# Cross attention: weighted values computed right behind a step's row phase, and their VectorE additions moved behind the row maxima

## Chip, cores and metric

One core of a Trainium2 chip runs the whole program. The metric is the device time in microseconds (us), the median of several runs. TensorE is called PE, its weight loads PEld, VectorE DVE, ScalarE ACT and GpSimd POOL.

## What is computed

A stream `x` of 32 batches of 64 tokens with 256 features goes through six layers. The first and the fourth are cross attentions with a context `ctx_512` of 1601 tokens and 128 features for each batch; the change touches these two alone.

```python
def _L0_xattn_ref(q, k, v, Wq, bq, Wk, bk, Wv, bv, Wo, bo):
    ...
    qh = (q @ Wq + bq).reshape(B, LQ, HEADS, D_K).transpose(0, 2, 1, 3)
    kh = (k @ Wk + bk).reshape(B, LKV, HEADS, D_K).transpose(0, 2, 1, 3)
    vh = (v @ Wv + bv).reshape(B, LKV, HEADS, D_K).transpose(0, 2, 1, 3)
    scale = 1.0 / np.sqrt(D_K)
    scores = jnp.einsum('bhqd,bhkd->bhqk', qh, kh) * scale
    attn = jax.nn.softmax(scores, axis=-1)
    out = jnp.einsum('bhqk,bhkd->bhqd', attn, vh)
    concat = out.transpose(0, 2, 1, 3).reshape(B, LQ, D_MODEL)
    return concat @ Wo + bo
...
    x = x + _L0_xattn_ref(_layernorm(x, axis=-1), ctx_512, ctx_512, L0_xattn_Wq, ...)
    x = x + _L0_attn_ref(...)
    x = x + _L0_ffn_ref(...)
    x = x + _L1_xattn_ref(_layernorm(x, axis=-1), ctx_512, L1_xattn_Wq, L1_xattn_Wkv, L1_xattn_Wo)
    x = x + _L1_attn_ref(...)
    x = x + _L1_ffn_ref(...)
```

There are 16 heads of 16 features, and the softmax subtracts the largest score of each row of a head before the exponential.

## The kernel before

`cross_attention` works through `STEPS` = 32 x 7 = 224 steps. Step `s` belongs to batch `u` and group `g` (`u, g = divmod(s, 7)`); a group is two tiles of 128 context tokens. Group 6 has one tile of 65 tokens, so its step is short. Each engine has its own program, a loop over the steps in a fixed order; the engines meet through semaphores alone.

PE does these blocks in step `s`, in this order:

- **Row phase (S)**, `scores(s)`: the scores of this step (L625) with the shift by the maximum (L631), and between them `largest` (L549), which computes in reduced precision the scores of the next batch, of which DVE takes the maxima. Both use 32 rows of the array for each of four strips. The phase opens with `largest` of the TRAIL strips 2 and 3, then come scores, and `largest` of the LEAD strips 0 and 1 stands near its end. ACT takes the exponentials of the scores (L805).
- **Keys (K)**, `project_keys` (L536), of the batch after: ACT copies them out (L708), POOL rounds them (L842).
- **Values (V)**, `project_values` (L568), of step `s + 2`: ACT copies them out (L716).
- In the last step of a batch **T**, `turn_maxes` (L557): the next batch's maxima are transposed and DVE copies them to `shift` (L920). For an even `u` above 0 the output projection **W**, `project_out` (L577), follows, which DVE adds to `x` (L966).
- **Weighted values (P)**, `weigh` (L596), of step `s - 1`: probabilities times values, 32 columns of the array for each strip. DVE's `gather` adds the result to `u_sb` (L974 in group 0, L977 in the others).

K, V, T, W, P and each of the four `largest` write to one of four PSUM banks, `misc_ps`, in turn. The list `ORDER`, filled by `step_ops(s)`, numbers these operations; number n uses bank n modulo 4, and `open_bank` makes PE wait until number n - 4 was read out by ACT (semaphore `act_free`) or DVE (`dve_free`):

```python
            def open_bank(op):
                if AT[op] >= NMB:
                    read_out(pe, ORDER[AT[op] - NMB])
                return bank(op)
```

The order of the blocks thus also says which read each block waits for. With M2, M3, M0, M1 for the four `largest` in program order, a plain step is M2, M3, M0, M1, K, V, P. K waits for the read of M2, V for M3, P for M0; in the next step M2 waits for M1, M3 for K (ACT), M0 for V (ACT) and M1 for P (DVE).

In group 0 the row phase also waits before its first score until DVE has copied `shift`: `read_out(pe, ("T", u))` (L619).

DVE takes in each step the four maxima (L910), then a share of the previous batch's division (`mask_odd` in group 2, `join_even` 3, `invert` 4, `divide` 5) or `keep_shift` in group 6, in the second cross attention also `later_tile` in the odd steps 3 to 25, and at last `gather`; `swap_halves` stands behind it in group 1.

Of the kernel before, what the change touches and what calls it, by code (L numbers as in the profile page):

```python
# [13 lines left out]
P = 128  # L14
# [203 lines left out]
def cross_attention(nc, tag, x_sb, ident, pair_mask, ctxT, wq, wk, wv, wo, bq, bv, bo, source=None, returned=None):  # L218
# [46 lines left out]
    def key_share(u, g):  # L265

        return (u + 1 + (g + 2) // NG, (g + 2) % NG)
# [4 lines left out]
    def step_ops(s):  # L272

        u, g = divmod(s, NG)
        ops = [("M", u + 1, g, j) for j in TRAIL + LEAD] if u + 1 < B else []
        if key_share(u, g)[0] < B:
            ops.append(("K",) + key_share(u, g))
        if s + 2 < STEPS:
            ops.append(("V", s + 2))
        if s in TURNED_AT:  # L280
            ops.append(("X", TURNED_AT[s]))
        if s in QUERIED_AT:
            ops.append(("Q", QUERIED_AT[s]))
        if s == 0 and bo is not None:
            ops.append(("C",))
        if g == NG - 1 and u + 1 < B:
            ops.append(("T", u + 1))
        if g == NG - 1 and u % 2 == 0 and u > 0:
            ops.append(("W", u // 2 - 1))
        if s > 0:  # L290
            ops.append(("P", s - 1))
        return ops

    ORDER = PROLOGUE + [op for s in range(STEPS) for op in step_ops(s)] + [("P", STEPS - 1), ("W", B // 2 - 1)]
# [8 lines left out]
    with ExitStack() as ctx:  # L303
# [170 lines left out]
        def _(pe):  # L474
# [5 lines that stand above are left out]
# [101 lines left out]
            def weigh(op):  # L581

                s = op[1]
                g = s % NG
                dst = open_bank(op)
                pe.wait_ge(exp_done, 2 * s + 2)
                if s == 0:
                    pe.wait_ge(filled, 1)
                read_out(pe, ("V", s))
                mine = tiles(g)  # L590
                for h, i in enumerate(mine):
                    for r in range(GROUPS):
                        c, half = r // 2, r % 2
                        at = ((h * KD + c) * 2 + half) * LQ
                        for j in range(QUADS):
                            ins = nc.tensor.matmul(  # L596
                                dst[j * 32:(j + 1) * 32, r * LQ:(r + 1) * LQ],
                                v_sb[0:keys(i), g, h, 4 * c + j, 2 * half:2 * half + 2, :].rearrange("p s d -> p (s d)"), probs[0:keys(i), s % 2, j, at:at + LQ],
                                start=h == 0 and r == 0, stop=h == len(mine) - 1 and r == GROUPS - 1, skip_group_check=True)
                ins.then_inc(misc_ready, 1)  # L600
# [77 lines left out]
            for s in range(STEPS):  # L678
                u, g = divmod(s, NG)
                scores(s)  # L680
                if key_share(u, g)[0] < B:
                    project_keys(("K",) + key_share(u, g))
                if s + 2 < STEPS:
                    project_values(("V", s + 2))
                if s in TURNED_AT:
                    turn_later(("X", TURNED_AT[s]))
                if s in QUERIED_AT:
                    project_queries(("Q", QUERIED_AT[s]))
                if s == 0 and bo is not None:
                    bias_row(("C",))  # L690
                if g == NG - 1 and u + 1 < B:
                    turn_maxes(("T", u + 1))
                if g == NG - 1 and u % 2 == 0 and u > 0:
                    project_out(("W", u // 2 - 1))
                if s > 0:
                    weigh(("P", s - 1))
            weigh(("P", STEPS - 1))
            project_out(("W", B // 2 - 1))

# [203 lines left out]
        def _(dve):  # L903
# [139 lines left out]
            for s in range(STEPS):  # L1043
                u, g = divmod(s, NG)
                if u + 1 < B:
                    for j in TRAIL + LEAD:
                        keep_max(("M", u + 1, g, j))
                if g == 2 and u > 0:
                    mask_odd(u - 1)
                if g == 3 and u > 0:  # L1050
                    join_even(u - 1)
                if g == 4 and u > 0:
                    invert(u - 1)
                if g == 5 and u > 0:
                    divide(u - 1)
                if s == 0 and bo is not None:
                    keep_bias(("C",))
                if g == NG - 1 and u + 1 < B:
                    keep_shift(("T", u + 1))
                if s in ADDED_AT:  # L1060
                    later_tile(ADDED_AT[s])
                if s == ROOTS_AT + 1 and returned is not None:
                    for j in range(1, TURNS):
                        invert_root(j)
                if g == NG - 1 and u % 2 == 0 and u > 0:
                    add_out(("W", u // 2 - 1))
                if s > 0:
                    gather(("P", s - 1))
                if g == 1 and u > 0:
                    swap_halves(u - 1)  # L1070
            gather(("P", STEPS - 1))
            swap_halves(B - 1)
            mask_odd(B - 1)
# [1838 lines left out]
```

## Time and profile before

| what | value |
|---|---|
| median of 3 runs | 3653.75 us (3653.49 to 3654.69) |
| profiled execution, its own time | 3656.24 us |
| its span | 3654.4 us, mean granted share of the PE clock 0.953 |
| PE busy | 3304.5 us (90%) |
| PE weight loads busy | 2671.3 us (73%) |
| DVE busy | 2496.6 us (68%) |
| ACT busy | 2194.2 us (60%) |
| POOL busy | 1474.0 us (40%) |

The span is that of the program's instructions on the core; the execution's own time holds it and the little that lies around it. The steps of the first cross attention lie from 46 to 973 us of the span, those of the second from 1629 to 2569 us. Matmuls overlap in the records, and the end of each is modelled; their starts are measured.

### The profile page before, as it was taken

The numbers are of one execution on the slowest core, as the hardware profiler recorded it, in microseconds if no ns is written. First come the engines' busy times: TensorE is split into PE (matmuls) and PEld (weight loads), VectorE is DVE, ScalarE is ACT, GpSimd is POOL, SyncE is SP. The second block draws the span as 40 slices with busy tenths as digits, with TensorE's granted clock in tenths as the row PEclk, the third lists the DMA queues.
The fourth block names the chain that finished last, engine by engine and source line by source line (L and its number), as shares of the span: only waits on it lengthen the run. The fifth ranks groups of instructions, "written<-read, shape, count | busy, mean of one in ns | idle before, by whom it ended". The sixth has DMA issues, their size and how long they took to land. (4 is left out here: it accounts for less than half of the span.)

```text
span 3654.4 us, 132188 instructions
## 1 busy us (share of the span) xinstructions
PE 3304.5 (90%) x56430; PEld 2671.3 (73%) x56431; DVE 2496.6 (68%) x4548; ACT 2194.2 (60%) x3465; POOL 1474.0 (40%) x1409
## 2 busy tenths in 40 slices
PE   9999999999886599979999999999867888888888
PEld 6888888888686466657888888888436666666667
DVE  5777777777545122248677777777669999999864
ACT  5666666666562122225766666666758888888632
POOL 4433333333132200045333333332029899999600
PEclk8999999999896799979999999999979999999989
DMA  2000001000005200011100100010001111111100
GB/s 80 31 31 31 31 31 40 31 31 22 11 2 215 101 32 31 30 65 58 33 30 31 31 31 31 31 40 4 27 17 50 44 47 46 45 47 47 36 25 23
DMA packets 60146, 147.51 MB, mean 40 GB/s; under 512 B 8210, under 2 KB 28466, under 8 KB 59218
## 3 DMA queue, kind: packets, MB, share of 16 engines
q1 hardware_dynamic: 56530, 131.04, 10.9%
q8 instruction: 442, 7.24, 0.8%
q0 software_dynamic: 3072, 8.39, 0.7%
q14 instruction: 102, 0.84, 0.1%
HBM read 122.63 MB, written 16.78 MB: 38 GB/s over the span
## 5 line engine op out<-in xcount | busy, mean ns | idle before, releaser
L805 ACT ACTIVATE x_probs<-x_score_ps 128x1024 f32<-128x1024 f32 (+1 forms) x896 | 815.1, 961 | 616.6 <-PE x_score_ps L631 588.7
L910 DVE TENSOR_REDUCE x_maxes<-x_misc_ps 128x1 f32<-128x512 f32 (+1 forms) x1792 | 1022.7, 627 | 36.3 <-PE x_misc_ps L549 30.7
L842 POOL CAST x_kT_hi<-x_kT 128x512 fp32r<-128x512 f32 (+1 forms) x448 | 254.2, 568 | 1141.1 <-ACT x_kT L708 1091.6
L2484 POOL TENSOR_TENSOR b_drive<-b_b_all,b_dtx 128x1024 f32<-128x1024 f32 x256 | 601.9, 2369 | 241.3 <-DVE b_dtx L2578 173.0
L2541 DVE TENSOR_TENSOR_SCAN b_state<-b_decay_ps,b_drive 128x512 f32<-128x512 f32 x512 | 598.9, 1212 | 33.9 <-POOL b_drive L2484 26.0
L625 PE MATMUL x_score_ps<-x_qz,x_kT 32*128 32x128 f32 x13312 | 592.9, 278 | 2.7 <-issue 2.2
L625 PEld LDWEIGHTS x_score_ps<-x_qz,x_kT 32*128 32x128 f32 x13312 | 502.3, 182 | 7.5 <-issue 5.1
L596 PE MATMUL x_misc_ps<-x_probs,x_v 128*32 128x64 f32 x26624 | 465.3, 221 | 1.1 <-issue 0.6
L596 PEld LDWEIGHTS x_misc_ps<-x_probs,x_v 128*32 128x32 f32 x26624 | 392.6, 110 | 78.6 <-issue 25.1
L2308 PE MATMUL b_turn_ps<-ident,b_state 128*128 128x128 f32 x2048 | 299.2, 288 | 153.7 <-DVE b_state L2541 97.3
L549 PE MATMUL x_misc_ps<-x_kT_hi,x_qz_hi 32*128 32x512 f32 (+1 forms) x2048 | 429.4, 405 | 5.5 <-DVE x_maxes L910 1.4
L2308 PEld LDWEIGHTS b_turn_ps<-ident,b_state 128*128 128x128 f32 x2048 | 230.7, 145 | 215.5 <-DVE b_state L2541 123.3
L2393 ACT ACTIVATE b_decay_ps<-b_dt,b_a_log 128x504 f32<-128x504 f32 x512 | 349.4, 683 | 63.2 <-DVE b_state L2541 62.6
L977 DVE TENSOR_TENSOR x_u<-x_misc_ps,x_u 128x256 f32<-128x256 f32 x384 | 162.9, 424 | 294.4 <-PE x_misc_ps L596 291.5
L631 PE MATMUL x_score_ps<-x_shift,x_ones 1*128 1x512 f32 (+1 forms) x1792 | 313.7, 456 | 0.5 <-issue 0.4
L2402 ACT ACTIVATE b_read<-b_turn_ps,b_c_turned 128x512 f32<-128x512 f32 x384 | 262.5, 684 | 72.5 <-PE b_turn_ps L2308 70.3
L716 ACT ACTIVATE x_v<-x_misc_ps 128x512 f32<-128x512 f32 (+1 forms) x448 | 260.4, 581 | 20.0 <-PE x_misc_ps L568 13.5
L708 ACT ACTIVATE x_kT<-x_misc_ps 128x512 f32<-128x512 f32 (+1 forms) x448 | 249.9, 558 | 16.0 <-PE x_misc_ps L536 15.4
L549 PEld LDWEIGHTS x_misc_ps<-x_kT_hi,x_qz_hi 32*128 32x128 f32 x2048 | 211.1, 185 | 64.3 <-DVE x_maxes L910 9.8
L394 POOL TENSOR_TENSOR x_raw_lo<-x_raw,x_raw_hi 128x512 fp32r<-128x512 f32 (+1 forms) x192 | 236.1, 1230 | 15.5
L568 PE MATMUL x_misc_ps<-x_wv_hi,x_raw_hi 128*128 128x256 f32 (+1 forms) x832 | 238.2, 286 | 0.0
L2314 PE MATMUL b_acc_ps<-ident,b_read 128*128 128x128 f32 x1536 | 235.0, 278 | 3.4 <-ACT b_read L2402 3.1
(318 smaller groups left out, 5777.6 us busy)
## 6 DMA issues: line engine op xcount, KB each, us to landing
x_raw<-in_ctxT SPq DMA_DIRECT2D x64, 800.5 KB, 4.5
b_b_all<-b_b_rows SPq DMA_DIRECT2D x128, 256.0 KB, 3.3
m_w<-in_m_w SPq DMA_DIRECT2D x16, 704.0 KB
m_w<-in_m_w SPq DMA_DIRECT2D x8, 768.0 KB
m_slot_rows<-m_zero SPq DMA_DIRECT2D x1, 4992.0 KB, 18.1
m_block_rows<-m_slot_rows SPq DMA_DIRECT2D x39, 128.0 KB, 2.0
m_slot_out<-m_out SPq DMA_DIRECT2D x39, 128.0 KB, 1.7
x<-in_x SPq DMA_DIRECT2D x4, 512.0 KB, 7.4
```

Of the source, the lines that this page charges most:

```text
L549: ins = nc.tensor.matmul(dst[:, m * kn:(m + 1) * kn], qz_hi[rows, b % 2, c, :, :].rearrange("p s q -> p (s q)"), kT_hi[rows, (b * NG + n) ...
L596: ins = nc.tensor.matmul(dst[j * 32:(j + 1) * 32, r * LQ:(r + 1) * LQ], v_sb[0:keys(i), g, h, 4 * c + j, 2 * half:2 * half + 2, :].rearran ...
L625: nc.tensor.matmul(score_ps[0:kn, j, n * P:(n + 1) * P], kT[rows, u % 2, c, cols(mine[h])], qz[rows, u % 2, c, :, :].rearrange("p s q -> p ...
L631: nc.tensor.matmul(score_ps[0:kn, j, 0:len(mine) * 2 * P], ones[j * 32:j * 32 + 1, 0:kn], shift[j * 32:j * 32 + 1, u % 2, :].rearrange("p ...
L716: nc.scalar.activation(v_sb[rows, g, 0:n, :, 0:4:3, :].rearrange("p a h s d -> p (a h) s d"), bank(op)[rows, 0:n * D].rearrange("p (a s d) ...
L805: nc.scalar.activation(probs[rows, s % 2, js, 0:n], score_ps[rows, js, 0:n], ACT.Exp).then_inc(exp_done, 1)
L910: nc.vector.tensor_reduce(maxes[:, c:c + m, j, k0 // NB], bank(op)[:, 0:m * even].rearrange("p (c k) -> p c k", c=m)[:, :, 0:kn], AX.X, AL ...
L2308: ins = nc.tensor.transpose(dst[:, c * P:(c + 1) * P], state[:, k % 2, c, i * P:(i + 1) * P], ident[:, :])
L2393: nc.scalar.activation(by_sequence(decay_ps[:, c % 2, :])[:, :, inside(p)], by_sequence(dt[:, p % 2, c, :])[:, :, inside(p)], ACT.Exp, sca ...
L2402: nc.scalar.activation(read[:, r, :], bank(use), ACT.Copy, scale=c_of(k, READ[r])).then_inc(act_free, 1)
L2484: nc.gpsimd.tensor_tensor(drive[:, h % 3, :, :], b_all[:, k % 2:k % 2 + 1, :].broadcast_to([P, 2, NB]), dtx[:, half * 2:half * 2 + 2, :], ...
L2541: nc.vector.tensor_tensor_scan(order(state[:, k % 2, c, :]), order(decay_ps[:, c % 2, :]), order(drive[:, h % 3, c % 2, :]), 0.0, ALU.mult ...
```

## The change

In a step, P (`weigh` of step `s - 1`) moves from the end to the place right behind the row phase, in `step_ops` and in PE's program. On DVE `gather`, and with it `swap_halves`, move from the end of the step to right behind the four maxima. ACT, POOL and SP keep their programs; the numbers that they wait for follow from `ORDER`. No instruction is added or taken away.

```diff
@@ step_ops(s)
         ops = [("M", u + 1, g, j) for j in TRAIL + LEAD] if u + 1 < B else []
+        if s > 0:
+            ops.append(("P", s - 1))
         if key_share(u, g)[0] < B:
             ops.append(("K",) + key_share(u, g))
...
             ops.append(("T", u + 1))
         if g == NG - 1 and u % 2 == 0 and u > 0:
             ops.append(("W", u // 2 - 1))
-        if s > 0:
-            ops.append(("P", s - 1))
         return ops
@@ tensor engine
                 scores(s)
+                if s > 0:
+                    weigh(("P", s - 1))
                 if key_share(u, g)[0] < B:
                     project_keys(("K",) + key_share(u, g))
...
                     project_out(("W", u // 2 - 1))
-                if s > 0:
-                    weigh(("P", s - 1))
@@ vector engine
                     for j in TRAIL + LEAD:
                         keep_max(("M", u + 1, g, j))
+                if s > 0:
+                    gather(("P", s - 1))
+                if g == 1 and u > 0:
+                    swap_halves(u - 1)
                 if g == 2 and u > 0:
                     mask_odd(u - 1)
...
-                if s > 0:
-                    gather(("P", s - 1))
-                if g == 1 and u > 0:
-                    swap_halves(u - 1)
```

A plain step is then M2, M3, M0, M1, P, K, V, and the reads that are waited for change with it: P waits for M2, K for M3, V for M0; in the next step M2 waits for M1, M3 for P (DVE), M0 for K and M1 for V (both ACT).

First place: PE, from the transposition T at the end of batch 1 of the first cross attention, a batch without W, to the first score of batch 2 (`x0` is the first cross attention). Before:

```order
L557 MATMUL x0_misc_ps<-ident,x0_neg_max 128x128 [waits x0_max_done,x0_dve_free]
L557 MATMUL x0_misc_ps<-ident,x0_neg_max 128x128
L596 MATMUL x0_misc_ps<-x0_probs,x0_v 32x64 [waits x0_act_free,x0_exp_done,x0_dve_free]
L596 MATMUL x0_misc_ps<-x0_probs,x0_v 32x64 x31
L549 MATMUL x0_misc_ps<-x0_kT_hi,x0_qz_hi 128x512 [waits x0_qz_hi_done,x0_kT_hi_done,x0_act_free] x2
L625 MATMUL x0_score_ps<-x0_qz,x0_kT 128x128 [waits x0_dve_free,x0_exp_done,x0_qz_done]
L625 MATMUL x0_score_ps<-x0_qz,x0_kT 128x128 x3
```

The same place after the change:

```order
L557 MATMUL x0_misc_ps<-ident,x0_neg_max 128x128 [waits x0_max_done,x0_dve_free]
L557 MATMUL x0_misc_ps<-ident,x0_neg_max 128x128
L549 MATMUL x0_misc_ps<-x0_kT_hi,x0_qz_hi 128x512 [waits x0_qz_hi_done,x0_kT_hi_done,x0_dve_free]
L549 MATMUL x0_misc_ps<-x0_kT_hi,x0_qz_hi 128x512 [waits x0_qz_hi_done,x0_kT_hi_done,x0_act_free]
L625 MATMUL x0_score_ps<-x0_qz,x0_kT 128x128 [waits x0_dve_free,x0_exp_done,x0_qz_done]
L625 MATMUL x0_score_ps<-x0_qz,x0_kT 128x128 x3
```

The 32 matmuls of P that stood between T and the row phase are gone from there, and the first score, which waits for the read of T (`x0_dve_free` in its list), follows T after two `largest`.

Second place: PE, `largest` of the LEAD strips and the block behind the row phase, in the short step (group 6) of the same batch. Before:

```order
L549 MATMUL x0_misc_ps<-x0_kT_hi,x0_qz_hi 128x66 [waits x0_kT_hi_done,x0_act_free]
L549 MATMUL x0_misc_ps<-x0_kT_hi,x0_qz_hi 128x66
L549 MATMUL x0_misc_ps<-x0_kT_hi,x0_qz_hi 128x66 [waits x0_kT_hi_done,x0_dve_free]
L549 MATMUL x0_misc_ps<-x0_kT_hi,x0_qz_hi 128x66
L631 MATMUL x0_score_ps<-x0_shift,x0_ones 65x256 x2
L536 MATMUL x0_misc_ps<-x0_raw_hi,x0_wk_hi 128x512 [waits x0_raw_lo_done,x0_w_lo_done,x0_dve_free]
L536 MATMUL x0_misc_ps<-x0_raw_hi,x0_wk_lo 128x512
```

The same place after the change:

```order
L549 MATMUL x0_misc_ps<-x0_kT_hi,x0_qz_hi 128x66 [waits x0_kT_hi_done,x0_act_free]
L549 MATMUL x0_misc_ps<-x0_kT_hi,x0_qz_hi 128x66
L549 MATMUL x0_misc_ps<-x0_kT_hi,x0_qz_hi 128x66 [waits x0_kT_hi_done,x0_act_free]
L549 MATMUL x0_misc_ps<-x0_kT_hi,x0_qz_hi 128x66
L631 MATMUL x0_score_ps<-x0_shift,x0_ones 65x256 x2
L596 MATMUL x0_misc_ps<-x0_probs,x0_v 32x64 [waits x0_act_free,x0_exp_done,x0_dve_free]
L596 MATMUL x0_misc_ps<-x0_probs,x0_v 32x64 x31
L536 MATMUL x0_misc_ps<-x0_raw_hi,x0_wk_hi 128x512 [waits x0_raw_lo_done,x0_w_lo_done,x0_dve_free]
L536 MATMUL x0_misc_ps<-x0_raw_hi,x0_wk_lo 128x512
```

The second strip's `largest` waited for DVE (its read of P) and now waits for ACT (its copy of V), and P stands where K stood.

Third place: DVE, groups 4 to 6 of batch 0's division, in the steps of batch 1. Before:

```order
L955 RECIPROCAL x0_recip<-x0_sums 128x128 [waits x0_sums_done]
L977 TENSOR_TENSOR x0_u<-x0_misc_ps,x0_u 128x256 [waits x0_dve_free,x0_misc_ready]
L910 TENSOR_REDUCE x0_maxes<-x0_misc_ps 128x1 [waits x0_misc_ready] x4
L960 TENSOR_TENSOR x0_oT<-x0_weighed,x0_recip 128x2x64 [waits x0_recip_done,x0_weighed_done]
L977 TENSOR_TENSOR x0_u<-x0_misc_ps,x0_u 128x256 [waits x0_dve_free,x0_misc_ready]
L910 TENSOR_REDUCE x0_maxes<-x0_misc_ps 128x2 [waits x0_misc_ready] x4
L917 TENSOR_REDUCE x0_neg_max<-x0_maxes 128x8 [waits x0_dve_free]
L920 CAST x0_shift<-x0_misc_ps 128x256 [waits x0_misc_ready]
```

The same place after the change:

```order
L977 TENSOR_TENSOR x0_u<-x0_misc_ps,x0_u 128x256 [waits x0_dve_free,x0_misc_ready]
L955 RECIPROCAL x0_recip<-x0_sums 128x128 [waits x0_sums_done]
L910 TENSOR_REDUCE x0_maxes<-x0_misc_ps 128x1 [waits x0_misc_ready] x4
L977 TENSOR_TENSOR x0_u<-x0_misc_ps,x0_u 128x256 [waits x0_dve_free,x0_misc_ready]
L960 TENSOR_TENSOR x0_oT<-x0_weighed,x0_recip 128x2x64 [waits x0_recip_done,x0_weighed_done]
L910 TENSOR_REDUCE x0_maxes<-x0_misc_ps 128x2 [waits x0_misc_ready] x4
L977 TENSOR_TENSOR x0_u<-x0_misc_ps,x0_u 128x256 [waits x0_dve_free,x0_misc_ready]
L917 TENSOR_REDUCE x0_neg_max<-x0_maxes 128x8 [waits x0_dve_free]
L920 CAST x0_shift<-x0_misc_ps 128x256 [waits x0_misc_ready]
```

The additions L977 stand right behind the four maxima; in group 6 one stands ahead of the maxima's last reduction L917 and of the copy of `shift` L920.

## Rows read from the trace of the kernel before

**Rows 1.** Busy time in the steps of the two cross attentions; columns as named.

```profile
core 0: us, PE busy (x) PEld busy (x) DVE busy (x) ACT busy (x) POOL busy (x), PEclk, DMA share, GB/s
47.00:973.00 926.00, 924.61 (x23865) 783.43 (x23865) 677.16 (x1416) 611.57 (x889) 329.40 (x472) 1.00 0.09 28
1629.00:2569.00 940.00, 933.92 (x23884) 788.23 (x23882) 695.35 (x1469) 623.89 (x911) 343.94 (x480) 1.00 0.10 31
```

**Rows 2.** Timeline, PE, a plain step; start, us, engine, line, operation, tiles.

```profile
612.68 0.50 PE L536 MATMUL x_misc_ps<-x_raw_hi,x_wk_hi 128*128 128x512 f32 x1
...
614.27 1.10 PE L596 MATMUL x_misc_ps<-x_probs,x_v 128*32 128x64 f32 x64
615.30 0.51 PE L549 MATMUL x_misc_ps<-x_kT_hi,x_qz_hi 32*128 32x512 f32 x2
...
616.87 0.50 PE L536 MATMUL x_misc_ps<-x_raw_hi,x_wk_hi 128*128 128x512 f32 x1
```

**Rows 3.** Timeline, PE and ACT, starts of group-1 steps, a middle and the last batch.

```profile
610.89 0.73 PE L549 MATMUL x_misc_ps<-x_kT_hi,x_qz_hi 32*128 32x512 f32 x2
...
610.47 0.60 ACT L708 ACTIVATE x_kT<-x_misc_ps 128x512 f32<-128x512 f32 x1
...
2525.62 0.75 PE L549 MATMUL x_misc_ps<-x_kT_hi,x_qz_hi 32*128 32x512 f32 x2
...
2527.42 0.50 PE L536 MATMUL x_misc_ps<-x_raw_hi,x_wk_hi 128*128 128x512 f32 x1
```

**Rows 4.** Timeline, PE and DVE, end of a batch without W.

```profile
576.59 0.39 PE L557 MATMUL x_misc_ps<-ident,x_neg_max 128*128 128x128 f32 x2
576.90 1.10 PE L596 MATMUL x_misc_ps<-x_probs,x_v 128*32 128x64 f32 x64
...
577.01 0.42 DVE L920 CAST x_shift<-x_misc_ps 128x256 fp32r<-128x256 f32 x1 [1.19 <-PE x_misc_ps L557]
```

**Rows 5.** Timeline, PE, DVE and ACT, a short step (group 6) and its ends.

```profile
601.20 0.28 PE L568 MATMUL x_misc_ps<-x_wv_hi,x_raw_lo 128*128 128x256 f32 x1
...
602.44 0.30 PE L549 MATMUL x_misc_ps<-x_kT_hi,x_qz_hi 32*128 32x66 f32 x2
...
603.09 0.37 PE L549 MATMUL x_misc_ps<-x_kT_hi,x_qz_hi 32*128 32x66 f32 x2
...
602.58 0.42 DVE L977 TENSOR_TENSOR x_u<-x_misc_ps,x_u 128x256 f32<-128x256 f32 x1 [1.12 <-PE x_misc_ps L596]
...
604.78 0.29 PE L568 MATMUL x_misc_ps<-x_wv_hi,x_raw_lo 128*128 128x256 f32 x1
...
605.11 0.60 ACT L716 ACTIVATE x_v<-x_misc_ps 128x512 f32<-128x512 f32 x1
```

**Rows 6.** Timeline, PE, row phases of the last batch, without keys and maxima.

```profile
968.03 0.48 PE L631 MATMUL x_score_ps<-x_shift,x_ones 1*128 1x512 f32 x2
968.44 0.33 PE L568 MATMUL x_misc_ps<-x_wv_hi,x_raw_hi 128*65 128x256 f32 x1
...
971.42 0.48 PE L631 MATMUL x_score_ps<-x_shift,x_ones 1*128 1x512 f32 x2
971.83 1.10 PE L596 MATMUL x_misc_ps<-x_probs,x_v 128*32 128x64 f32 x64
```

**Rows 7.** Timeline, DVE, the four maxima of the group-0 step that PE starts at 607.12.

```profile
607.65 2.48 DVE L910 TENSOR_REDUCE x_maxes<-x_misc_ps 128x1 f32<-128x512 f32 x4
```

**Rows 8.** Timeline, first step of the second cross attention: T, then a row phase.

```profile
1628.61 0.49 PE L549 MATMUL x_misc_ps<-x_kT_hi,x_qz_hi 32*128 32x512 f32 x2
1628.72 0.42 DVE L920 CAST x_shift<-x_misc_ps 128x256 fp32r<-128x256 f32 x1 [5.33 <-PE x_misc_ps L557]
...
1629.26 1.00 PEld L625 LDWEIGHTS x_score_ps<-x_qz,x_kT 32*128 32x128 f32 x30 [0.47 <-issue]
...
1630.85 0.50 PE L536 MATMUL x_misc_ps<-x_raw_hi,x_wk_hi 128*128 128x512 f32 x1
```

**Rows 9.** Timeline, DVE, a step with `later_tile` in the second cross attention.

```profile
1707.97 1.23 DVE L986 SCALAR_TENSOR_TENSOR x<-x_back,m_prob,x 128x256 f32<-128x256 f32 x2
```

## The prediction

> **What bounds the kernel now.** I read the busy times of the two stretches first. PE is busy 924.6 of 926 us in the steps of the first cross attention and 933.9 of 940 in those of the second, no other engine over 74% [rows 1]. The change moves blocks on PE and DVE there and nothing elsewhere, so the question is what PE waits for. The Trainium skill's page "Perfetto Trace Analysis", section "Identifying the Most-Contended Engine", says that matmul busy time is no good measure here, since matmuls are pipelined. The rows bear that out: going by the busy row nothing could be gained and the sum below would be 13 us higher, while starts show real waits. I therefore read the timeline by the starts of blocks.
>
> A plain step takes 4.19 us from one K to the next [rows 2]: 1.03 of it are P, and 1.57 the row phase S, from its first `largest` to K. Nothing waits in it. The reader is to see three places where this changes.
>
> *Group 1.* P of group 6 has half the matmuls, so the row phase of group 1 starts some 0.45 us early. M3 there waits until ACT has copied K. ACT's K ends at 610.47 + 0.60 = 611.07, .05 before PE goes on; the merged row of `largest` lasts 0.73 us in a middle batch and 0.75 in the last that has it, instead of 0.51 [rows 2, 3]. The phase takes 2527.42 - 2525.62 = 1.80 us instead of 1.56: a stall of 0.24 us. The two attentions have 60 such steps (batches 1 to 30); in about five early ones of the second attention other waits stand in its place.
>
> *End of a batch.* T starts at 576.59, P behind it at 576.90, and the next row phase 1.03 us later [rows 2]; DVE's copy of `shift` is ready at 577.01 + 0.42 = 577.43 [rows 4]. P hides that copy.
>
> *Short step.* The addition of P by DVE ends at 602.58 + 0.42 = 603.00, which is 0.56 us behind the start of the row phase at 602.44, and M1 goes at once behind it (its matmul's start at 603.09, after a load) [rows 5]. So M1 is already bound by the read that it waits for.
>
> **What the change costs, part by part.** Number of instructions and queue of each engine stay the same; only order and releasers move.
>
> 1. *The blocks themselves.* A step has the same blocks, and PE goes through the same three kinds of array use (strips of 32 rows, the whole array, strips of 32 columns) once each. What a block costs behind another one must be priced for S to P, P to K and V to S in place of S to K, V to P and P to S. Without `largest`, S goes over to V 968.44 - 968.03 = 0.41 us after its last start and to P 971.83 - 971.42 = 0.41 [rows 6]. Equal prices for two different followers: I take 0 for all three pairs. P to K is not in the trace. Bounds: the loads of a whole-array block could follow at no extra price or at double; T to P costs 576.90 - 576.59 = 0.31 [rows 4] where its two matmuls alone need about 0.22 (the merged row of 0.39 less the 0.28 of one matmul is the 0.11 from start to start), so a changeover is about 0.09 us, and P to K lies within 0.09 either side. It happens 428 times: +/-39 us at the very ends. The Trainium skill, "TensorEngine Tiling (Array Packing)", section "Key Properties", says that a change of the tiling mode drains TensorE. By that rule P to K is a changeover like P to S, and the sum is again 0; no row shows that pair, so it stays a rival.
>
> 2. *Group 1.* M3 now waits for P's read by DVE. P stands at 1.57 us of the step of group 0 and, with half the matmuls, is done by about 2.3. DVE's four maxima of such a step end at 607.65 + 2.48 = 610.13, 3.0 us after its start [rows 7], the addition behind them 0.42 later [rows 5], at 3.45; the next row phase starts at 4.19 - 0.45 = 3.74. K's copy is now waited for by M0 and V's by M1, which stand about 1 us inside the phase. The stall goes: 55 x 0.24 = -13.2 us. Bounds: 60 x 0.24 = -14.4 and, if DVE is late in some, -11.
>
> 3. *End of a batch without W.* T now stands directly before the row phase. Its first score waits for the copy of `shift`, which ends 0.84 us after T's start; the phase would start at 0.31 [rows 4]. How soon PE goes on, and whether the wait is paid in full, is shown once: at the first step of the second attention the row phase starts at 1628.61, the copy ends at 1628.72 + 0.42 = 1629.14, the first load of a score comes at 1629.26, and K at 1630.85, so this phase took 2.24 us against 1.57 [rows 2, 8]. Loads 0.65 late made it 0.67 longer, all paid. Here: 0.84 + 0.12 = 0.96, less 0.31, is 0.65; with the same 0.01 to 0.02 on top 0.66. Behind the score the whole phase is queued on PE, and the exponentials on ACT behind it. Of the 31 T in each attention 15 have W behind them, which takes longer than the copy and hides it (W itself waits for nothing new); 16 have not. 32 x 0.66 = +21.1 us. Bounds: 0.53, if PE goes on at once behind the copy (+17.0), and 0.68 (+21.8).
>
> 4. *Short step.* M1 of group 6 now waits for ACT's copy of V, the last block of the step before. V's last matmul at 601.20 ends at 601.48, and the block behind it, now P, starts 1.03 us before 602.44, at 601.41 [rows 5]. With the row phase in that place, V is done 0.07 us after the phase starts. A free ACT starts 0.04 us after a V (604.78 + 0.29 = 605.07, then 605.11) and takes 0.60 [rows 5], to 0.71 us. DVE's read ended at 0.56. M1, and the block behind the phase with it, comes 0.15 later. In plain steps, whose phase has twice the scores, M1 stands later in it, and the copy is in time. The 62 steps of group 6 (batches 0 to 30): 62 x 0.15 = +9.3 us; lower bound 0.10 each (+6), if part of it fits under the last shift matmuls.
>
> 5. *DVE behind the maxima.* Addition and shuffle now run while PE computes K and V and DVE had nothing. What stood behind them (maxima of the next step) starts as soon as PE gives them. Only where DVE is the late one does this matter: the odd steps 3 to 25 of the second attention, where `later_tile` begins at 1707.97 and keeps DVE for two microseconds [rows 9]. The second stretch is 940 - 926 = 14 us longer than the first [rows 1], part of it for six transpositions that the first has elsewhere; some 11 us are such stalls. The work ahead of the next maxima stays the same, `gather` included, so the late steps stay late; DVE's sequence starts at most 0.2 us earlier in each of 12 steps. I take -1 us; bounds 0 and, if all of it went, -11.
>
> Sum: +21.1 + 9.3 - 13.2 - 1.0 = +16.2 us. Against the profiled execution's 3656.2 us that is 3672.4. That execution stands 2.5 us above the median of the runs shown, so I set the median at 3653.75 + 16.2 = 3670.0 us, 0.44% slower. Its own range, with the bounds of 2 to 5 short of the all-or-nothing end of 5, is 3662 to 3675.
>
> **Rivals.**
>
> *A: it comes out even.* The copy of `shift` and that of V come sooner than I read them (lower bounds, +23.0), and the stalls of the second attention go largely (-9) beside group 1 (-13.2): +0.8, so 3655. For it: DVE's addition no longer stands directly before the maxima on which P waits. Against it: the same work still stands there, and the wait for `shift` has been seen paid in full [rows 8]. Even with half of it the sum is within 7 us, and a measurement of this kernel can tell about 0.2%, 7.3 us, from no change.
>
> *B: faster, by the price of P to K.* If a K behind P saved the whole 0.09 us changeover, 428 x 0.09 = 38.5 us would go: 3631. It turns the sign from 0.055 us a block on, (16.2 + 7.3) / 428. For it: no row shows the pair. Against: S to V and S to P are equal [rows 6].
>
> *C: much slower, by the same price.* A K that costs 0.09 us more behind P gives 3708.
>
> *D: the change does not do what it says.* If group 1 kept its stall, since DVE's read of P came as late as ACT's of K, the sum would be +29.4 and the time 3683. That takes DVE 0.25 us later than my 3.45 us; from 3.7 on it begins to cost.
>
> **How the numbers follow.** Forecast, 3662 to 3675: 0.57. A: 0.22. B: 0.08. C: 0.04. D, and the forecast with more of it, up to 3690: 0.09. Faster by over 0.2% is B with a little of A, 0.10; within 0.2% is the rest of A and the lower edge, 0.20; slower 0.70. The range leaves out B and C and most of D: 3653 to 3680.
>
> **What the changed kernel's profile would show.** Group-1 phases of 1.56 us, their first two `largest` as long as elsewhere (step 2). In the 16 batches a gap of 0.65 us between the first `largest` of a batch and the first load of its scores, with DVE's L920 as releaser, and none in those with W (3). P after a short phase 0.15 us later than K stands there now, M1's load released by ACT's L716 (4). P to K with the same 1.03 us from P's first matmul (1). If that last number is another one, the prediction is wrong by 428 times the difference; if the gap behind T is shorter, by 32 times.

## The result, and the profile after

The changed kernel takes 3663.35 us (median of 19 runs, 3659.18 to 3665.91), the kernel before 3654.53 us in the same session (19 runs, 3649.88 to 3661.95). The ratio is 1.0021, 95% interval 1.0014 to 1.0029: slower by some 8 us. The direction was forecast, the size (+16.2 us) was about double. One execution of `p_first_in_0`, of 6200.84 us, is left out of its ratio below.

The span of the profiled execution goes from 3654.4 to 3664.1 us. Below I compare the stretch that the change touches, from the start of the first row phase of an attention to that of its last: in the first attention 926.4 us before and 928.2 after, in the second 940.5 and 947.1. Together that is +8.4 us, as much as the measured change. The rest of the span is 1787.5 us before and 1788.8 after. Over the 14 kernels profiled for this document it lies anywhere from 1781.0 to 1791.4 (the first row phase starts at 43 to 49 us), though no edit but that of the warm-up touches it. So the whole spans of two single profiles can differ by up to 10 us for reasons outside the change, and I compare the two stretches instead.

The busy times of the two stretches after, to set beside [rows 1] (columns: us, then busy us and count of PE, PEld, DVE, ACT, POOL, the PE clock as a share, DMA share, GB/s):

```profile
47.00:973.00 926.00, 922.99 (x23766) 781.08 (x23764) 666.46 (x1413) 645.90 (x887) 330.65 (x473) 1.00 0.09 28
1629.00:2569.00 940.00, 927.70 (x23580) 782.48 (x23580) 683.33 (x1461) 653.11 (x905) 344.56 (x481) 1.00 0.10 31
```

PE's idle time is 3.0 and 12.3 us, where it was 1.4 and 6.1. The clock is at its full 2.4 GHz level in both, so nothing below comes from it.

**The end of a batch without W.** The timeline of the changed kernel at such a place, to set beside [rows 4, 8] (start us, us, engine, line, operation; in brackets the idle time before and its releaser):

```profile
580.26 0.24 PEld L557 LDWEIGHTS x_misc_ps<-ident,x_neg_max 128*128 128x128 f32 x2
...
580.67 0.50 PE L549 MATMUL x_misc_ps<-x_kT_hi,x_qz_hi 32*128 32x512 f32 x2
580.77 0.42 DVE L920 CAST x_shift<-x_misc_ps 128x256 fp32r<-128x256 f32 x1 [1.28 <-PE x_misc_ps L557]
...
581.32 1.00 PEld L625 LDWEIGHTS x_score_ps<-x_qz,x_kT 32*128 32x128 f32 x30 [0.47 <-issue]
581.35 1.12 PE L625 MATMUL x_score_ps<-x_qz,x_kT 32*128 32x128 f32 x27 [0.18 <-DVE x_shift L920]
```

From the first `largest` (580.67) to the first load of a score (581.32) it is 0.65 us, and DVE's copy ends at 581.19, between the two. Over all 32 such batches the median row phase is 2.23 us, where it was 1.576. Behind W it is 1.57 as before.

**Group 1.** The row phase of the step behind it:

```profile
585.08 0.50 PE L549 MATMUL x_misc_ps<-x_kT_hi,x_qz_hi 32*128 32x512 f32 x2
...
586.63 0.88 PE L596 MATMUL x_misc_ps<-x_probs,x_v 128*32 128x64 f32 x48
```

It takes 586.63 - 585.08 = 1.55 us instead of 1.80 [rows 3], and the merged row of the first two `largest` lasts 0.50 us instead of 0.73. The medians over 30 batches are 1.561 and 1.565 in the two attentions.

**The short step,** group 6:

```profile
576.72 0.30 PE L549 MATMUL x_misc_ps<-x_kT_hi,x_qz_hi 32*128 32x66 f32 x2
...
576.82 0.60 ACT L716 ACTIVATE x_v<-x_misc_ps 128x512 f32<-128x512 f32 x1
...
577.61 0.27 PE L549 MATMUL x_misc_ps<-x_kT_hi,x_qz_hi 32*128 32x66 f32 x1
577.81 1.10 PE L596 MATMUL x_misc_ps<-x_probs,x_v 128*32 128x64 f32 x64
578.84 0.50 PE L536 MATMUL x_misc_ps<-x_raw_hi,x_wk_hi 128*128 128x512 f32 x1
```

ACT's copy of V ends at 577.42, 0.70 us into the phase (0.71 forecast), and P starts at 577.81: the phase is 1.09 us long instead of 0.95. P to K is 578.84 - 577.81 = 1.03, so a K behind P costs what a row phase behind P did.

**What was not in the sum.** In the second attention, while POOL still gathers late tiles, PE stops in the middle of P:

```profile
1679.67 1.00 POOL L853 DMA_INDIRECT x_back<-m_slot_out,m_slot  x1 [0.15 <-issue]
...
1679.79 0.76 PE L596 MATMUL x_misc_ps<-x_probs,x_v 128*32 128x64 f32 x39
1680.97 0.60 PE L596 MATMUL x_misc_ps<-x_probs,x_v 128*32 128x64 f32 x25 [0.43 <-issue]
```

39 of the 64 matmuls, then a gap that no semaphore ends ("issue"), then the other 25, 0.30 us after the gather's row ends at 1680.67. Beside 16 of the 24 such gathers in the second attention of the changed kernel PE has a stop of 0.36 us or more, and each ends 0.28 to 0.35 us behind the gather's row. What PE waited for in this stretch, by the view of waits (engine, output, line, releaser: us, times, longest), in the changed kernel:

```profile
PE x_misc_ps L596 <- issue: 5.5, 16, 0.4
PE x_misc_ps L596 <- DVE x_maxes L910: 3.2, 5, 1.2
```

And in the kernel before, over the same 1632 to 1770 us:

```profile
PE x_score_ps L625 <- issue: 0.9, 4, 0.3
PE x_misc_ps L549 <- DVE x_u L977: 0.7, 3, 0.3
PE x_misc_ps L596 <- issue: 0.6, 2, 0.4
PE x_misc_ps L549 <- issue: 0.6, 1, 0.6
```

Gaps without a releaser are there in both, in the row phase before and in P after. And the kernel before has such gaps all over its two attentions, the changed kernel not. One of them, from the timeline of the kernel before:

```profile
812.00 0.46 PE L596 MATMUL x_misc_ps<-x_probs,x_v 65*32 65x64 f32 x20
812.39 0.75 PE L549 MATMUL x_misc_ps<-x_kT_hi,x_qz_hi 32*128 32x512 f32 x2
812.64 0.71 PE L625 MATMUL x_score_ps<-x_qz,x_kT 32*128 32x128 f32 x7
813.85 0.72 PE L625 MATMUL x_score_ps<-x_qz,x_kT 32*128 32x128 f32 x16 [0.50 <-issue]
```

To price them I took the length of each block in steps 7 to 216 of an attention, less the median of its kind (block, group, with or without W), and summed what is over by more than 0.06 us. I also counted PE's records (matmuls, weight loads and its waits and branches) from the start. 12 of the 16 such blocks in the first attention of the kernel before, 5.2 of 5.8 us, hold a record whose number is 193 modulo 256; in the second, behind step 29, where the gathers are over, 4.3 of 5.1 us hold number 113 modulo 256. The instruction queue of the DMA moved 442 packets of 16 KB during the run. The Trainium skill, "Trainium Architecture — The Big Picture", section "The software stack", gives 64 bytes for an instruction. By this figure a packet holds 256 of them, an estimate; 442 such packets would hold 113,152, near PE's 117,795 records. I call these places packet ends.

The account of the 8.4 us, from these block lengths (us, both attentions, before to after):

| part | before | after | change |
|---|---|---|---|
| row phase behind T without W, 32 x (2.230 - 1.576) | | | +20.9 |
| row phase of group 6, 62 x (1.093 - 0.953) | | | +8.7 |
| row phase of group 1, 60 x (1.563 - 1.805) | | | -14.5 |
| stalls at packet ends, away from the gathers | 9.5 | 0.1 | -9.4 |
| POOL's gathers in steps 0 to 29 of the second attention (next section) | 7.3 | 11.3 | +4.0 |
| the rest | | | -1.3 |
| sum | | | +8.4 |

### The profile page after: what moved, and what is told of

Same layout as the page of the kernel before. It is cut to its first block and busy times, and to the rows that moved or that the text cites. A ratio compares the mean times of both kernels' runs of the same rounds, so it can differ in the third digit from the quotient of the medians.

```text
span 3664.1 us, 132188 instructions
## 1 busy us (share of the span) xinstructions
PE 3306.1 (90%) x56430; PEld 2671.8 (73%) x56431; DVE 2478.0 (68%) x4548; ACT 2265.2 (62%) x3465; POOL 1474.2 (40%) x1409
## 5 line engine op out<-in xcount | busy, mean ns | idle before, releaser
L549 PE MATMUL x_misc_ps<-x_kT_hi,x_qz_hi 32*128 32x512 f32 (+1 forms) x2048 | 417.4, 406 | 2.0 <-DVE x_maxes L910 1.0
L568 PE MATMUL x_misc_ps<-x_wv_hi,x_raw_lo 128*128 128x256 f32 (+1 forms) x832 | 234.0, 281 | 0.0
```

The lines of the kernel that those rows point to most:

```text
L549: ins = nc.tensor.matmul(dst[:, m * kn:(m + 1) * kn], qz_hi[rows, b % 2, c, :, :].rearrange("p s q -> p (s q)"), kT_hi[rows, (b * NG + n) ...
L568: ins = nc.tensor.matmul(dst[0:keys(i), h * D:(h + 1) * D], part[:, b % 2, cols(i)], w[:, :], start=m == 0, stop=m == 2)
```

## The experiments

The theory at this point: three waits as forecast, +15.1 us in all, and two effects of PE's instruction supply, which the change moves as well. Rivals: the three waits do not add up, part of each being paid elsewhere; or the stalls of the second attention are DVE's lateness behind `later_tile`, as I had forecast.

### One group at a time

P, and `gather` with it, moved in the groups of a list `FORWARD` alone (this edit for each of the three programs that hold the order):

```diff
+    FORWARD = (0,)
...
-                if s > 0:
+                if s > 0 and g in FORWARD:
                     weigh(("P", s - 1))
...
+                if s > 0 and g not in FORWARD:
+                    weigh(("P", s - 1))
```

`p_first_in_0`, with `FORWARD = (0,)`:

> P and its gather stand behind the row phase in the steps of group 0 alone; all other steps keep the order of the kernel before. Theory (the moved time is a sum of three separate waits): only the group-1 stall goes, 60 times 0.24 us and the little that sat beside it, so 13 to 16 us less than before; the row phase of group 1 at 1.56 us, that of group 0 after a batch without W at 1.57, that of group 6 at 0.95. Rival (group 1's stall was worth little, because PE would have stood for its own instructions or for DVE there): 0 to 5 us less than before.

`p_first_in_6`, with `(6,)`:

> P and its gather behind the row phase in the steps of group 6 alone. Theory: only the wait of the first score for the copy of shift comes, 32 times 0.6 to 0.66 us, so 19 to 21 us more than before; group 1 keeps its stall (1.80 us), group 6 its 0.95. Rival (the wait is partly paid already, by other stalls at the batch's end): 10 to 15 us more.

`p_first_in_5`, with `(5,)`:

> P and its gather behind the row phase in the steps of group 5 alone, so that V is the last block ahead of the row phase of group 6. Theory of the prediction: 62 times 0.15 us, 9.3 us more than before. Rival (the profile after shows +0.14 for the median step but +5.6 in all, since steps with another stall pay nothing more): 5 to 6 us more. Group 0 and group 1 as before.

`p_last_in_6`, with `(0, 1, 2, 3, 4, 5)`:

> P behind the row phase in groups 0 to 5, and last, as before, in group 6, so that P hides the copy of shift. Theory: the changed kernel less 19 to 21 us, that is 10 to 12 us less than the kernel before; group 1 at 1.56, group 0 at 1.57 after every batch, group 6 at 1.10. Rival (the 9 us that the changed kernel loses come from something spread over all steps, such as POOL's period in the second attention): at most 6 us less than before.

Measured (the change against the kernel before: that of the steps in the trace, and the time by the ratio with its interval):

| kernel | waits by their medians | packet ends (before: 9.5) | steps | time |
|---|---|---|---|---|
| `p_first_in_0` | -14.5 | 13.4 | -5.1 | -5.8, ratio 0.9984 (0.9969 to 1.0000) |
| `p_first_in_6` | +20.9 | 13.4 | +23.8 | +24.8, 1.0068 (1.0055 to 1.0081) |
| `p_first_in_5` | +8.7 | 13.7 | +10.6 | +9.9, 1.0027 (1.0016 to 1.0039) |
| `p_last_in_6` | -5.8 | 8.0 | -4.9 | -4.7, 0.9987 (0.9979 to 0.9996) |

Each wait came and went alone, at the size of the changed kernel: group 1 at 1.565 in `p_first_in_0`, group 0 at 2.23 in `p_first_in_6`, group 6 at 1.09 in `p_first_in_5`, and the others as before. Yet the time of the first is 9 us short of its theory, and its interval reaches 1.0000: my number for it failed, and the rival's "0 to 5" nearly holds, for another reason than it gave. The difference is the third column. With P moved in one group alone there are more stalls at packet ends, +4 us each (a shift of the stream alone changes this sum by 3.7 us, as shown below, so not all of that need be the order's); in `p_first_in_0` 4 us of stalls come in the steps with gathers as well. In `p_first_in_6` the new ones stand where the order has P, row phase and P in a row (P of step 4 ends step 5, P of step 5 follows the next row phase): in 23 steps P of group 6 is longer by more than 0.06 us, 9.4 us together, and in every one the packet end lies in that P. Of the 21 that lie away from the gathers, the first late record is number 193 (first attention) or 113 (second) itself in 20. `p_first_in_5` is within 1 us of the 9.3 forecast, but by two errors that cancel: its group-6 phases grow by 5.6 us in sum, as the rival had it, and packet ends add the rest. `p_last_in_6` has rid itself of the 32 waits for `shift`, but gains 13.2 us of steps on the changed kernel and not 21, for packet ends cost 8.0 us again; the "at most 6 us" of its rival held. So the three waits add up, and a fourth term changes from placement to placement.

### Leave POOL's late gathers out

DVE then adds stale data, so `x` is not the reference's; the kernel shows only what the gathers cost.

```diff
-                if s in RETURNED_AT:
-                    t = RETURNED_AT[s]
-                    pool.wait_ge(second_added, t - BACK + 1)
-                    fetch(t, s % 2, late_returned[t % BACK])
...
-                dve.wait_ge(late_returned[t % BACK], 32 * (t // BACK))
```

> The changed kernel with POOL's 24 late gathers (fetch, L853, two a tile in steps 0 to 23 of the second attention) left out, and DVE's wait for them; DVE still adds, from stale data, so the tiles 4 to 15 of x are not the reference's. Theory (PE gets no new instructions while POOL issues an indirect gather): the stalls of P and S in steps 7 to 55 of the second attention, 13.8 us in the trace of the changed kernel, go to under 3 us, and the time falls by 11 to 16 us. Rival of the prediction (DVE is late there because of later_tile, which stays): the stalls stay, within 3 us.

> The same left out of the kernel before. Theory: its 12.4 us of stalls in steps 7 to 55, which stand in the row phase there, go as well, and it falls by 10 to 15 us. Rival: DVE is late in the kernel before, later_tile stays, and so do the stalls, within 3 us.

Changed kernel without them: ratio 0.9997 to the kernel before (0.9988 to 1.0006), so 8.8 us less than the 1.0021 of the whole one. The steps of the second attention go from 947.1 to 935.5. Kernel before without them: ratio 0.9986 (0.9977 to 0.9995), 5.1 us less; its steps from 940.5 to 932.8. The time falls by less than the theory's lower bound in both (8.8 and 5.1 for 11 and 10), its cause is shown all the same: the 8.2 us that P had too much in the changed kernel are 0, and "issue" is gone from the view of waits of this stretch, whose first line is

```profile
PE x_misc_ps L596 <- DVE x_maxes L906: 3.7, 5, 1.2
```

But the rival is right too, for the other half: 5.9 us of stalls stay in steps 7 to 29 of the changed kernel, 6.2 in the kernel before. In the changed kernel they are, by the view of waits, mostly DVE's: P, which now waits for the read of M2, stands until DVE is through `later_tile` and the first maximum.

```profile
1678.50 1.13 DVE L982 SCALAR_TENSOR_TENSOR x<-x_back,m_prob,x 128x256 f32<-128x256 f32 x2
...
1680.23 2.45 DVE L906 TENSOR_REDUCE x_maxes<-x_misc_ps 128x1 f32<-128x512 f32 x4
...
1680.94 1.10 PE L596 MATMUL x_misc_ps<-x_probs,x_v 128*32 128x64 f32 x64 [1.18 <-DVE x_maxes L906]
```

The first of the four maxima ends 2.45 / 4 = 0.61 us after 1680.23, at 1680.84, and P starts 0.10 later. In the kernel before without gathers another block pays: the last `largest` of the row phase, M1, waits until DVE, behind `later_tile`, has added P. In steps 10, 12, 14, 18, 20, 24 and 26 it starts 0.05 to 0.06 us behind the end of that addition. Step 12:

```profile
1678.31 0.41 DVE L973 TENSOR_TENSOR x_u<-x_misc_ps,x_u 128x256 f32<-128x256 f32 x1
...
1678.78 0.50 PE L549 MATMUL x_misc_ps<-x_kT_hi,x_qz_hi 32*128 32x512 f32 x1 [0.36 <-DVE x_u L973]
```

The price of the gathers is read from steps 0 to 29 of the second attention, which hold them all: 135.8 us before and 128.5 without gathers, 141.0 after and 129.7 without. They cost PE 7.3 us before and 11.3 after, and the change makes that +4.

### Move the packet ends

56 in place of 24 warm-up transpositions at the start:

```diff
-    WARM = 24
+    WARM = 56
```

> The kernel before with 56 warm-up transpositions in place of 24 at the very start: PE's stream of instructions is the same and lies 64 records later. It begins some 5 to 7 us later. Theory (the scattered stalls without a wait in the row phase, 5.2 us in the first attention, come where PE runs on to its next 256 instructions, a 16 KB packet of the instruction queue, right behind P): they stand in other steps than before, again at one and the same record number modulo 256 (193), their sum between 2 and 10 us. Rival (they come from what runs beside them in those steps, such as the context's loads): they stand in the same steps and blocks as before, 57, 71, 85, 87, 183, 201, at another number modulo 256.

> The changed kernel with 56 warm-up transpositions in place of 24. The kernel before has 13 stalls of 5.2 us at record 193 modulo 256 in its first attention, and 10 of some 2.7 us when the stream was moved by 64; the changed kernel has 0.1 us of them. Theory (the order of the blocks, not the place of the 256-record ends, keeps it free: K and V, slow to read, follow P, and PE's next 256 instructions come in time): under 1 us again. Rival (the changed kernel had luck with where the ends fell): 2 to 5 us.

Each was executed once: 3646.53 us for the kernel before, 3659.56 us for the changed one. The warm-up opens both attentions, so the stream lies 64 records later in the first and 128 in the second. In the kernel before the stalls moved to other steps: those of the first attention that hold record 193 modulo 256 are now steps 44, 51, 57, 59, 90, 149, 155, 157, 173, 195 and 203, 2.9 us together, and of the six that I had named only step 57 is still one of them. The number stayed, 193 and in the second attention 113 (another 2.9 us behind step 29). So it is the place in PE's stream. The changed kernel, shifted, has none of them in either attention, again; only the gathers' stalls in P stand as they were, 8.2 us. So at both positions of the stream its order keeps it free of them. What they cost the kernel before does depend on the position: 5.2 + 4.3 = 9.5 us as it is, 2.9 + 2.9 = 5.8 shifted. Its steps are 5.1 us shorter so, those of the changed kernel 0.7. In the shifted pair the change costs 12.8 us in the steps and 13.0 by the two single times, not 8.4: a part of the small result is where the packet ends happened to lie in the kernel before.

In 15 of the 16 longest gaps at packet ends in the kernel before, PE goes on 1.24 to 1.60 us after the last packet of the instruction queue has ended, which is 2.2 to 2.9 us after it began; at packet ends taken together the median is 2.6 and 3.7 us. The packet was late there, by the records of the DMA. That is as far as these runs go: what sets the moment at which a packet is asked for, none shows.

### T ahead of V

`step_ops` has the same move.

```diff
                 if key_share(u, g)[0] < B:
                     project_keys(("K",) + key_share(u, g))
+                if g == NG - 1 and u + 1 < B:
+                    turn_maxes(("T", u + 1))
                 if s + 2 < STEPS:
                     project_values(("V", s + 2))
...
-                if g == NG - 1 and u + 1 < B:
-                    turn_maxes(("T", u + 1))
```

> The changed kernel with T between K and V in group 6, so that V lies between T and the next row phase. V and the changeover last 0.71 us, and the copy of shift is 0.65 late without it. Theory: the 32 stalls of 0.66 us go, 19 to 21 us less than the changed kernel, 10 to 13 us less than the kernel before, if T itself is ready (neg_max, now behind the addition on DVE, in time 0.8 us after P's end). Rival (neg_max is late, and T waits in all 62 steps for 0.2 us or more): under 10 us less than the changed kernel. Third (PE's own supply takes the place of the slack): 13 to 15 us less, as P last in group 6 gave.

Ratio 0.9989 (0.9980 to 0.9998), so 11.7 us less than the changed kernel; in its steps 16.6 less. The place in its timeline:

```profile
569.49 0.40 PE L557 MATMUL x_misc_ps<-ident,x_neg_max 128*128 128x128 f32 x2
569.64 0.36 PE L568 MATMUL x_misc_ps<-x_wv_hi,x_raw_hi 128*128 128x256 f32 x1
...
569.93 0.42 DVE L920 CAST x_shift<-x_misc_ps 128x256 fp32r<-128x256 f32 x1 [0.59 <-PE x_misc_ps L557]
...
570.53 0.50 PE L549 MATMUL x_misc_ps<-x_kT_hi,x_qz_hi 32*128 32x512 f32 x2
570.54 0.71 PE L625 MATMUL x_score_ps<-x_qz,x_kT 32*128 32x128 f32 x12
```

The scores start 0.01 us behind `largest`, the copy has ended 0.18 us earlier, and T does not wait. All 32 stalls are gone: the row phases of group 0 take 21.7 us less. Some 5 us come back: T and V of group 6 together 1.3, the row phases of group 1 1.6, P of group 6 1.6, and small sums elsewhere. Theory's number was 19 to 21 and is missed; the rival (a late T) is wrong; the third case, 13 to 15, lies between the time and the steps, and is nearest in size.

### The gather behind P

POOL issues the gather of a step before it rounds keys, and waits for P first:

```diff
+                if s in RETURNED_AT:
+                    t = RETURNED_AT[s]
+                    pool.wait_ge(second_added, t - BACK + 1)
+                    if s > 0:
+                        made(pool, ("P", s - 1))
+                    fetch(t, s % 2, late_returned[t % BACK])
                 if key_share(u, g)[0] < B:
                     round_keys(*key_share(u, g))
...
-                if s in RETURNED_AT:
-                    t = RETURNED_AT[s]
-                    pool.wait_ge(second_added, t - BACK + 1)
-                    fetch(t, s % 2, late_returned[t % BACK])
```

> The changed kernel; in the second attention POOL issues the gather of a step (fetch, L853) ahead of its rounding of keys and right behind P, so that it runs while PE does K and V, 18 records in 1.6 us, and not while PE does P, 128 in 1.03. Nothing is left out. Theory: the 8.2 us of stalls in P of the steps 7 to 23 go, those that later_tile causes (6.6 us, which stayed when the gathers were left out) stay, so 6 to 9 us less than the changed kernel. Rival (PE waits as long, whatever block it is in, as 1 us of gather is 1 us without new instructions): P is whole, and V or the row phase longer by the same, within 2 us of the changed kernel.

Ratio 1.0003 (0.9994 to 1.0012), 6.6 us less than the changed kernel; the steps of the second attention 8.3 less. The theory's 6 to 9 held.

```profile
1670.71 0.28 PE L568 MATMUL x_misc_ps<-x_wv_hi,x_raw_hi 128*128 128x256 f32 x1
...
1670.79 0.99 POOL L853 DMA_INDIRECT x_back<-m_slot_out,m_slot  x1 [2.17 <-PE x_misc_ps L596]
...
1671.51 0.53 PE L549 MATMUL x_misc_ps<-x_kT_hi,x_qz_hi 32*128 32x512 f32 x2
```

The gather runs beside V, and V and the row phase behind it take what they take elsewhere. P has no stall left (8.2 us to 0), and the steps 0 to 29 take 132.8 us, 3.1 more than without gathers. A microsecond of gather is thus not a microsecond of PE. My reading of the two placements is that PE gets no new instructions while the gather is issued, and that it costs what PE would have read meanwhile beyond what it already holds; no run shows this supply itself. The Trainium skill, "Perfetto Trace Analysis", section "DMA Instruction — SWDGE (GPSIMD)", says that such a row of POOL is the writing of the descriptors, and not the transfer. The trace of the changed kernel agrees: the row is 1.00 us long, and the gathers land 2.9 us (median) after they are issued. PE goes on 0.30 us behind the end of the row, 1.30 us after its start.

### Both, and a third

> T between K and V in group 6 and the gather right behind P, both on the changed kernel. If the two are independent: 16.6 us less for T, as the steps of its trace showed, and what the gather alone gives, together 21 to 26 us less than the changed kernel and 12 to 17 less than the kernel before. If not: as turn_ahead_of_values alone, 12 to 17 less than the changed kernel.

Ratio 0.9953 (0.9939 to 0.9967): 3635.5 us beside 3653.7 of the kernel before, 17 us less, and 24.8 us less than the changed kernel by the two ratios. Both ranges held, the second at its edge. `p_last_in_6` and `turn_ahead_of_values` beat the kernel before by 4 to 5 us; this version beats it by most.

The third edit puts `lower(TRAIL)` ahead of `largest` of the LEAD strips in group 6:

```diff
+                if g == NG - 1:
+                    lower(TRAIL)
                 if not last:
                     for j in LEAD:
                         largest(("M", u + 1, g, j))
-                lower(TRAIL)
+                if g < NG - 1:
+                    lower(TRAIL)
```

> As turn_and_fetch, and in group 6 PE does the shift of strips 2 and 3 (lower) ahead of largest of strips 0 and 1, so that M1, which waits for the copy of V there, stands later. Theory: the 62 row phases of group 6 go from 1.09 to 0.95 or 1.00 us, 5 to 9 us less than turn_and_fetch. Rival (the wait was for the bank of M1, and M1 as the last of the phase starts no sooner, so P behind it does neither): within 2 us of turn_and_fetch.

Ratio 0.9953 (0.9939 to 0.9966), the same. The steps of its one trace are 4.5 us shorter than those of `turn_and_fetch`, in groups 1 and 5 and not in group 6, and the medians of the times do not show it. The row phase of group 6 stays at 1.093 us:

```profile
598.32 0.60 ACT L719 ACTIVATE x_v<-x_misc_ps 128x512 f32<-128x512 f32 x1
...
598.87 0.51 PE L549 MATMUL x_misc_ps<-x_kT_hi,x_qz_hi 32*128 32x66 f32 x3
...
599.30 1.10 PE L596 MATMUL x_misc_ps<-x_probs,x_v 128*32 128x64 f32 x64
```

V's copy ends at 598.92 and P starts 0.38 us later; in the changed kernel it was 577.81 - 577.42 = 0.39, with two `lower` among the matmuls between. What stands between the copy and P is M1 itself and the way to P, and those two matmuls cost nothing there. The rival held.

## Why the prediction was right in sign and wrong in size

Two terms failed. The sum had nothing for waits inside typical steps ("Nothing waits in it"), and there were stalls at packet ends of 9.5 us, which the change removed. Step 5 put the late steps of the second attention down to DVE alone and took -1 us; POOL's gathers, which it does not name, added 4.0 us there. That the median, 3663.35 us, lies within the forecast's own 3662 to 3675 is luck: two missed terms of opposite sign left it just inside the lower edge. The sign follows from the three waits, +15.1 us, which were foreseen.

*Step 1, changeovers at 0: right.* P to K is 1.03 us, like P to the row phase before, in 428 places; rivals B and C fall with that.

*Step 2, group 1: right.* Forecast -13.2, measured -14.5 by 60 medians. Rival D did not come.

*Step 3, T without W: right.* Forecast +21.1, measured 20.9, with the 0.65 us gap and the releaser as forecast.

*Step 4, short step: right in its place, a little large in its size.* Forecast +9.3, 62 x 0.14 = 8.7 measured; V's copy and its end are where they were worked out to be. The kernel before had some 3 us of other stalls in these phases, which are gone, and the sum of all group-6 phases rose by 5.5 only.

*Step 5, DVE behind the maxima: here the prediction failed.* "Some 11 us are such stalls" put all that is long in the early second attention down to DVE and `later_tile`. With the gathers left out about 6 us of it stay, before as after, and most of that is DVE's, so "the late steps stay late" held for them. The other part, 7.3 us before, went with POOL's gathers, during which PE stops although it waits for no semaphore. The change moved P, which takes 128 records in 1.03 us, under them, and they cost 11.3 us. Forecast -1 for this stretch; the gathers alone made +4.

*The term that was taken as nothing: packet ends.* "Nothing waits in it" is true of the plain step that I showed and not of all. Blocks of the kernel before that were too long at packet ends cost 9.5 us, nearly all in the row phase right behind P. With K and V between P and the row phase they are gone, -9.4 us. This is the larger part of the miss: the forecast sum of 16.2 less 9.4, plus 4.0 + 1.0 for the gathers in place of my -1, less 2.1 for the three waits (17.2 forecast, 15.1 measured) and 1.3 unexplained, is 8.4. It is also the term whose size rests on chance: with the stream shifted the kernel before pays 5.8 us there instead of 9.5. I had read the starts of typical steps; what is too long in one step of eight (50 blocks in 2 x 210 steps) does not show there.

That the changed order is free of stalls at packet ends and that of the kernel before is not, is shown by the shifted pair, and `p_first_in_6` shows them move with its P; why the order "row phase, P, K, V" is free and "P, row phase" is not, is argued only: K and V are 18 records in 1.6 us, time for a packet to come. Of rival A, the even outcome, the sum came half way, by a mechanism that it did not name.

## What to carry to other kernels

Where PE does many small matmuls, its instructions acted here like a resource with its own deadline: put the blocks with few, long instructions right behind the block with many short ones, and keep indirect gathers of POOL beside the former. Before costing a reordering, list the blocks that are longer than the median of their kind, not only the medians, and see whether gaps that no semaphore ends come at one record number modulo 256. A one-bank rotation turns a reordered block into someone else's wait; the waits found by bank number, block by block, were right to 0.01 us each.

## What the runs showed of the hardware that I had not expected

- PE's blocks were up to 1.0 us too long in the kernel before at a fixed place modulo 256 records, and went on 1.24 to 1.60 us after a 16 KB packet of the instruction queue had ended. This cost 0.1 to 13.7 us over two attentions, by the order of the blocks, and in one order 9.5 or 5.8 us by the position of the stream.
- In the gather shown (1.00 us of POOL), PE does 39 matmuls of P and their loads, and stops until 0.30 us after it; 16 of the 24 gathers of the changed kernel have such a stop, which ends 0.28 to 0.35 us behind them. The 24 cost 11.3 us. Beside K and V they cost 132.8 - 129.7 = 3.1 us.
- Two `lower` matmuls behind the last `largest` of group 6 cost nothing: with or without them it is 0.38 to 0.39 us from the end of V's copy to P.
